# Upper halves of every second probability tile copied to a buffer of their own by GpSimd

## What is computed

```python
f = _l2norm(feats.reshape(B * N, C))
scores = jnp.matmul(f, f.T) / TEMPERATURE
attn = jax.nn.softmax(scores, axis=-1)
feats_att = jnp.matmul(attn, f)
feats_fcm = f * W_BLEND + feats_att * (1.0 - W_BLEND)
return _l2norm(feats_fcm.reshape(B, N, C))
```

## Time and profile before

| | us |
|---|---|
| median of 3 runs | 980.53 |
| lowest and highest | 980.06, 985.04 |
| the profiled execution | 982.02 |
| its span on the core | 980.2 |
| granted TensorE clock, mean of the span | 0.983 |

### The profile page before, as it was taken

How to read it: one execution, slowest core, us unless ns; L and a number is a source line. 1 busy time by engine, 2 the same in 40 slices (tenths; PEclk the granted TensorE clock), 3 DMA queues, 4 the chain that set the end, 5 groups by cost and what they waited for, 6 DMA issues and landing times.

```text
span 980.2 us, 31296 instructions
## 1 busy us (share of the span) xinstructions
PE 911.3 (93%) x13700; PEld 549.1 (56%) x13700; DVE 809.5 (83%) x953; ACT 650.1 (66%) x1179; POOL 139.9 (14%) x109
## 2 busy tenths in 40 slices
PE   1979599999999999999999999999999889999895
PEld 1434255556786666678668667766865444444231
DVE  6044888989889898988988989899889888999874
ACT  0112568778877887787878787788776656555552
POOL 3021400000000000000000000000003631556633
PEclk9999889999999999999999999999999899999998
DMA  9996000000000000000000000000000000000001
GB/s 188 213 213 130 1 2 3 2 3 2 3 2 3 2 3 2 3 2 2 3 3 2 3 2 3 2 3 2 3 2 2 3 2 2 1 11 12 11 23 32
DMA packets 21015, 22.30 MB, mean 23 GB/s; under 512 B 3168, under 2 KB 19680, under 8 KB 20880
## 3 DMA queue, kind: packets, MB, share of 16 engines
q1 hardware_dynamic: 20256, 19.47, 10.2%
q0 software_dynamic: 448, 0.67, 0.4%
q10 hardware_dynamic: 176, 0.18, 0.1%
HBM read 18.21 MB, written 2.10 MB: 21 GB/s over the span
## 4 chain that ended last, share of the span: by engine, by line
PE 79%; DVE 10%; DMA 5%; POOL 3%; issue 2%; ACT 1%; SPq 0%; POOLq 0%; DVEq 0%; ACTq 0%
PE ps L405 31%; PE ps L420 22%; PE ps L433 11%; DMA ring<-in_x_dram 4%; PE ps L341 3%; PE ps L483 3%; DVE ring L782 3%; PE ps L555 2%; PE ps L544 2%; DVE ring L900 1%; POOL stat L248 1%; PE ps L443 1%; DVE f L730 1%; ACT combT L650 1%; PE ps L561 1%
## 5 line engine op out<-in xcount | busy, mean ns | idle before, releaser
L782 DVE TENSOR_TENSOR ring<-ring 128x1024 f16<-128x1024 f32 x512 | 607.1, 1233 | 52.7 <-ACT ring L676 51.3
L676 ACT ACTIVATE ring<-ps 128x1024 f32<-128x1024 f32 x512 | 519.3, 1020 | 146.0 <-PE ps L405 145.9
L405 PE MATMUL ps<-big 64*64 64x512 f16 x6144 | 387.0, 379 | 1.3 <-ACT ring L676 1.3
L405 PEld LDWEIGHTS ps<-big 64*64 64x64 f16 x6144 | 223.4, 107 | 117.5 <-issue 5.2
L420 PE MATMUL ps<-ring,fs 64*64 64x512 bf16 x4096 | 285.9, 387 | 0.9
L420 PEld LDWEIGHTS ps<-ring,fs 64*64 64x64 f16 x4096 | 150.2, 106 | 80.2 <-issue 6.7
L433 PE MATMUL ps<-ring,fs 64*64 64x512 f16 x2048 | 163.4, 380 | 14.6 <-DVE ring L782 13.9
L248 POOL TENSOR_TENSOR stat<-stat,cst 128x8 f32<-128x8 f32 x24 | 43.4, 1813 | 702.7 <-DVE stat L811 656.4
L433 PEld LDWEIGHTS ps<-ring,fs 64*64 64x64 f16 x2048 | 73.7, 107 | 55.2 <-issue 18.6
L676 ACT ACTIVATION_READ_ACCUMULATOR ring<-ps 128x1 f32 x512 | 101.6, 198 | 0.0
L341 PE MATMUL ps<-ring,weff 128*128 128x512 f32 x128 | 59.0, 617 | 21.1 <-DVE weff L734 14.2
(11 more groups left out here) (109 smaller groups left out, 445.5 us busy)
## 6 DMA issues: line engine op xcount, KB each, us to landing
ring<-in_x_dram SPq DMA_DIRECT2D x16, 1024.0 KB, 18.9
out_dram<-h SPq DMA_DIRECT2D x16, 128.0 KB, 2.4
f<-in_L_tok_W_dram SPq DMA_DIRECT2D x2, 288.0 KB, 5.1
xedge<-in_x_dram POOLq DMA_DIRECT2D x2, 128.0 KB, 7.3
wall<-in_L_ffn_w_dram POOLq DMA_DIRECT2D x2, 128.0 KB, 7.2
cst<-consts_dram ACTq DMA_DIRECT2D x1, 144.0 KB, 2.3
w2s<-in_L_ffn_w_dram POOLq DMA_DIRECT2D x2, 64.0 KB, 8.7
fs<-consts_dram ACTq DMA_DIRECT2D x1, 32.0 KB, 3.2
```

The costliest lines, as they stand in the source:

```text
L405: last = mm(bank(SLOT_BANK[slot_of(s)] + r)[m:m + 64, :], of_k[r][:, 128 * k + m:128 * k + m + 64], of_q[r][:, q0 + 512 * r:q0 + 512 * r + ...
L676: a(probs[:, s % 8, :], bank(SLOT_BANK[slot_of(s)], 2), ACT.Exp, accum_out=rowsum[:, s:s + 1]).then_inc(s_pr, 1)
L782: tt(probs_lo[:, s % 8, :], probs[:, s % 8, :], probs[:, s % 8, :].bitcast(BF16)[:, 1:2 * QC:2], ALU.subtract).then_inc(s_lo, 1)
```

## The change

POOL copies, for every odd tile, the upper 16 bits of the 1024 probabilities of each partition from `probs` (step of two 16-bit elements) to `high_part`, a new buffer of four tiles of 128x1024 bfloat16, contiguous. A copy waits for the exponential (s_pr) and for the crossed wide sums of the tiles that used the place before (s_ph), and raises s_hi. The wide sums of odd tiles read `high_part`; those of even tiles read `probs` as before. PE waits for s_hi before each group of wide sums, ACT before it overwrites an odd tile. DVE's program is unchanged. There are 256 copies.

```diff
+        high_part = sb("high_part", [128, 4, QC], BF16)
...
+            def high_copy(s):
+                pool.wait_ge(s_pr, s + 1)
+                if s >= 8:
+                    pool.wait_ge(s_ph, s // 4 - 1)
+                nc.gpsimd.tensor_copy(high_part[:, s // 2 % 4, :],
+                                      probs[:, s % 8, :].bitcast(BF16)[:, 1:2 * QC:2]).then_inc(s_hi, 1)
+
+            for s in range(1, NS - NT, 2):
+                high_copy(s)
+
...
             for t in range(PAIRS):
+                high_copy(NS - NT + 2 * t + 1)
                 for i in range(EARLY):
...
+                pe.wait_ge(s_hi, 2 * g + 2)
                 for s in range(4 * g, 4 * g + 4):
                     for m in (0, 64):
                         for r in range(2):
                             half = 1 - r if crossed else r
-                            last = mm(bank(4 + half)[m:m + 64, :], fs[64 * r:64 * r + 64, s % NT, m:m + 64],
-                                      probs[64 * r:64 * r + 64, s % 8, :].bitcast(BF16)[:, 1024 * half + 1:
-                                                                                       1024 * half + 1024:2],
+                            rows = slice(64 * r, 64 * r + 64)
+                            if s % 2:
+                                high = high_part[rows, s // 2 % 4, 512 * half:512 * half + 512]
+                            else:
+                                high = probs[rows, s % 8, :].bitcast(BF16)[:, 1024 * half + 1:1024 * half + 1024:2]
+                            last = mm(bank(4 + half)[m:m + 64, :], fs[rows, s % NT, m:m + 64], high,
                                       start=(s % NT == 0 and not crossed), stop=False, skip_group_check=True)
...
                 if s >= 8:
                     act.wait_ge(s_ph, s // 4 - 1)
+                    if s % 2:
+                        act.wait_ge(s_hi, s // 2 - 3)
                     act.wait_ge(s_lo, s - 7)
```

More of the change, by code:

```diff
@@ L161, in tower @@
         s_ss, s_rt, s_fs, s_ftr, s_ftev, s_ftev2 = (sem(n) for n in ("s_ss", "s_rt", "s_fs", "s_ftr", "s_ftev", "s_ftev2"))
-        s_sc, s_pr, s_lo, s_straight, s_ph, s_pv, s_oev = (sem(n) for n in ("s_sc", "s_pr", "s_lo", "s_straight", "s_ph", "s_pv", "s_oev"))
+        s_sc, s_pr, s_hi, s_lo, s_straight, s_ph, s_pv, s_oev = (sem(n) for n in ("s_sc", "s_pr", "s_hi", "s_lo", "s_straight", "s_ph", "s_pv", "s_oev"))
         (s_at, s_att, s_g, s_gsq, s_ss1, s_rn, s_gn, s_res, s_mean, s_cen, s_hsq, s_var, s_rstd, s_ln, s_hhi, s_hs,
```

## The result

The changed kernel takes 1120.2 us (median of 4 runs, 1115.55 to 1121.69) against 982.27 us of the kernel before in the same series (980.06 to 985.04): a ratio of 1.1395, 95% interval 1.1346 to 1.1443. It is slower by 138 us. The profiled execution has a span of 1117.8 us.

What follows compares the result with a forecast made beforehand. PE bounds the kernel, DVE close behind; copies excluding DVE's low parts make DVE the bound. Middle passes +92.5, first +17.4, last +28, tail 0: +138 us on 982.0 is 1120, less 1.5 to the median about 1118 us; range 1030 to 1195.

Steps and rivals of the forecast that it cites:

- the last pass's ends of 13 and 41 us: Last loop pass: time added if a copy costs DVE 0.47 or 1.13 us, the bounds of its price.
- the third rival: POOL's strided 16-bit copy runs at its two-input rate, 5 us a step, PE waiting on s_hi: about 1570 us; 4%.
- The price of a copy: DVE time lost to each POOL copy through their mutual exclusion: 0.82 us, bounds 0.47 and 1.13.
- Middle passes: Passes 1 to 6 of the attention loop: DVE becomes the bound at 3.10 us a step, 602 against 509.5 us, +92.5.
- First pass: First loop pass: DVE's sum of low parts, blocking and 32 copies gives 105.5 against 88.1 us, +17.4.
- Last pass: Last loop pass: 32 copies, +23 us on DVE, plus 5 us for copies queued behind POOL's other work: +28 us.
- Tail: After the loop: no copies there, so 0 us change.
- PE's gain: Contiguous reads in PE's wide sums: 0.02 us a step, 5 us or 0.5% at most, only while PE is the bound.
- PE's waits: PE waits about 1 us at every second step's low sums, released by DVE; waits on POOL would disprove the sum.
- the copies are ready in time: Middle passes: POOL gets the port after at most one low part, before PE wants the copy two matmul groups later.
- No exclusion: Rival: a plain one-input copy costs DVE under 0.34 us, PE stays the bound: 978 us; 6%.
- Whole instructions: Rival: DVE and POOL instructions exclude each other for their whole length, 3.61 us a step: 1230 us; 7%.

Runs made afterwards that it cites:

- Experiment 1: Changed kernel with all copies made, but PE neither waits for them nor reads them; all wide sums read the tiles: 1111.19 us, ratio 1.132.
- experiment 5: Changed kernel with half as many copies: only the fourth tile of each group is copied and read from the buffer; 1017.0 us, ratio 1.032.
- experiment 7: Changed kernel with a copy only every fourth step, which PE neither waits for nor reads: 990.73 us, ratio 1.008.
- experiment 11: Two runs of the changed kernel: without the last pass's copies 1089.95 us, ratio 1.1076; without the first pass's copies 1103.99 us, ratio 1.1235.
- experiment 3: Changed kernel with no copies: buffer zeroed once, all four tiles of a group read contiguously from it; 978.15 us, ratio 0.9937.
- experiment 2: Changed kernel with POOL writing zeros (memset) instead of copying, all waits and contiguous reads kept: 992.61 us, ratio 1.0097.
- experiment 9: Changed kernel with DVE's low part a plain one-input conversion, subtraction left out, all copies and waits kept: 1035.93 us, ratio 1.052.
- experiment 10: Changed kernel with the one-input low part and all copies, but PE neither waits for them nor reads them: 980.3 us, ratio 0.9976.

## Why the prediction was right, point by point

It said 1118 us and 1030 to 1195; measured were 1120.2. Two of its side figures don't follow from their own terms, and nothing rests on them: the last pass's ends of 13 and 41 us come out as 17 and 38, and the third rival's 1570 us as about 1580.

**The price of a copy: right.** 0.82 us was taken from one cast of 584 elements, scaled by length; 0.83 was measured with 1024 and 0.40 with 512 elements. That the cast was chosen over the two-input additions, by the number of inputs and the byte step, made the number; the additions gave 1.13.

**Middle passes: right.** 602 us forecast, 601.35 measured. Experiment 1 shows the cause alone. Experiments 5 and 7 show the threshold, the price that a step bears before it gets longer: at half the price per step it is 2.692, at a quarter 509.5 us as without copies.

**First pass: right.** +17.4 forecast, +16.5 measured; the copies in it cost 16.9 us by experiment 11. PE resumed at 122.96 (forecast 123.4), as its timeline shows:

```profile
122.96 0.64 PE L439 MATMUL ps<-ring,fs 64*64 64x512 bf16 x4 [9.17 <-POOL high_part L250]
```

**Last pass: right in size, wrong in its parts.** +28 forecast, +23.0 measured. DVE's 23 us were somewhat too many (its busy time rose by 119.3 - 97.5 = 21.8), and the 5 us of queueing too few: with memsets, which exclude nothing, the last pass was 8.6 us longer. Why the two don't simply add is not shown; a PE that waits gives DVE time to run down its work.

**Tail: missed.** Forecast 0, measured +6.8 us. It goes with the granted clock (0.92 for 0.97), and experiment 3 has it (+6.6) without any copy. The forecast put the tail at 0 because it has no copies, and left the clock there out; why the clock was lower isn't shown. The last pass's -5 and the tail's +6.8 cancelled in the total, so the hit of 2 us is in part luck; 5 us either way would be the fair claim.

**PE's gain: right.** 0.02 us a step for two tiles; 0.023 by experiment 2 (2.633 - 2.610), 0.043 for four. For the change it is worth 4 us in the middle passes, and it could not collect them.

**What was said on PE's waits: half wrong.** I expected them at DVE's low parts alone and wrote that waits for POOL would make the sum wrong in kind. Half of them were for copies (37.0 us in 48 waits), and the sum held: DVE was busy 600.3 of 601.4 us, so who holds PE changed nothing. The sentence "the copies are ready in time" was wrong for these 48 of the 192 steps, by up to 0.8 us; it went unpunished only because DVE was the bound. In experiment 9, where DVE is not, the same lateness cost 34 us in the middle passes (545.1 against 510.8 in experiment 10).

**The rivals.** No exclusion (978 us) would have been right with a write-only POOL instruction, in the middle passes. Whole instructions (1230 us): the rule of the Trainium skill ("SBUF — State Buffer", "Who interferes with whom") names the right pair and the right condition, a low part with two inputs against a POOL instruction that reads and not against one that only writes, and experiments 1 and 2 agree (604.1 and 505.3 us). That the pair is held for the whole instruction is more than was measured: 0.83 us of a copy that takes 1.03 alone.

## What to carry to other kernels

Before giving idle GpSimd a reading job beside a busy vector engine, look for any place in the trace where the two overlap, compare their durations with those alone, and add the job's length to the vector engine's step: up to the slack it is free (0.35 us here), and what goes beyond the slack is added to every step. The length to add is a little less than the job's own: 0.83 us here for a copy of 1.03. A helper that another engine waits for must also be judged by when its result comes, not only by its load: with a quarter of the copies the price of the exclusion was nil and the wait, with the lower clock after it, still cost 30 us. And cap such a change by its best case first; here it was 0.5%.

## What was not expected of the hardware

- A GpSimd copy asked for while DVE was at its eighth or a later low part in a row, the PSUM copy before them counted in, was shut out until DVE paused, for the low part under way and up to three more (5.04 to 5.08 us for 1.03), in 19 of 19 cases. With 6 or fewer it was always let in after the running one. The cause is open.
- A conversion f32 to f16 with one input on DVE, both in SBUF, excludes GpSimd's reads too: the copies took 1.57 us instead of 1.03.
- The tail took 164 to 166 us at a granted clock of 0.92 to 0.93 instead of 157.6 at 0.97, with the same program, in the changed kernel and in experiments 2 and 3, the last without copies. In experiment 10 it took 158.3 us at 0.97, in experiments 7 and 11 (no last pass) 161 at 0.94, and without the first pass's copies 168.3 at 0.89: by and large, the lower the clock, the longer the tail.
